# Joining two small TensorE products into one in a software-pipelined audio block

## The chip, the cores and the metric

The kernel runs on one core of a Trainium2 chip, in one launch. The metric is the device time of that launch in microseconds (us). Five instruction streams run side by side: PE (TensorE; its weight loads are listed apart as PEld), DVE (VectorE), ACT (ScalarE), POOL (GpSimd) and SP (SyncE, which here only issues DMAs). They meet through semaphores that are written out by hand.

## The reference, cut to what matters

The input is 16 sequences of 120000 samples, cut into 938 frames of 128 samples. A DCT of each frame gives 938 tokens of 128 channels; then come a decayed linear-attention layer with its MLP, and a layer with one expert for each sequence. Only the attention's scan matters here:

```
for each token t, per head (4 heads of 32 channels):
    A = lam[:, None] * A + k_t[:, None] * v_t[None, :]     # state, 32 x 32
    z = lam * z + k_t
    S_t = q_t . A ;  Z_t = q_t . z
att = S / Z
```

## The kernel before, in words

One sequence is one item `b` of a software pipeline over 16 items. Each round of the pipeline works on up to four items at different stages, and in every engine's block a function `body` writes out by hand in which order the steps of the items are issued. Tokens lie in tiles of 128 (`TILES` is 8), each tile being two blocks of 64 (`BLK`). Everything is in f32; on the trace one f32 product is two MATMUL records and two LDWEIGHTS records (a transpose is one of each).

The scan is done by blocks. Inside a block, TensorE builds the decayed scores of keys and queries (`pairs`, L1061: lines L1076, L1081 and L1086), and `scan` (L1102) multiplies them with the values (L1125). Between blocks the state is carried: for each of the first 14 blocks (`NST`) and each head, `us` (L1051) computes the block's contribution to the state, a product of the keys decayed to the block's end, `kcT` (128 tokens of a tile x 32 channels, the stationary operand), with the values. So that a product over all 128 token rows of a tile sums one block only, the values are held in two copies: `v[0]` is zero in the rows of the second block and `v[1]` in those of the first. The result goes into one PSUM bank, where element (e, i) of block i stands at column 14 e + i. DVE runs the decayed scan over the blocks in one instruction (`chain`, L813), POOL spreads it to all heads (`states`, L441), and `scan` uses it (L1118).

In each round PE issues `us` between `zts` (L1048, the denominators) and `dcts` (L1004) of the next item; behind these stand transposes (L1009), `w2s` (L1148), `ats` (L1164), `pairs(b, 2)`, and three `f1s` (L1170). SP hands the values over with two DMAs (`hand_v`, L350), before a copy of the stage's tokens (`hs`), the queries' spreads (`qx`), the way of the denominators through DRAM (`rz_dram`, `zq`) and a second copy of `hs`.

Of the kernel before, what the change touches and what calls it, by code (L numbers as in the profile page):

```python
# [10 lines left out]
P = 128  # L11
HEADS = 4
HD = P // HEADS
# [6 lines left out]
BLK = P // 2  # L20
# [31 lines left out]

def program(nc, A, out):
    B, _, full = A["xT"].shape
    T = full + 1
    TAIL = A["xtail"].shape[1]
    E = A["fc1T"].shape[0]
    TILES = -(-T // P)
    PADT = TILES * P
# [8 lines left out]
    NST = NBLK - 1  # L68
    KT = TILES - 1

    ctx = ExitStack()
    with ctx:
# [3 lines left out]
        def sb(name, *shape, dt=F32):  # L76
            return ctx.enter_context(nc.sbuf_tensor(name, [P, *shape], dt))
# [47 lines left out]
        v_f, gate_f = sb("v_f", TILES, P), sb("gate_f", PADT)  # L125
# [7 lines left out]
        kcT = sb("kcT", KT, P)  # L133
        rms_row, to_end, ends = sb("rms_row", P), sb("to_end", P), sb("ends", P)
        af = sb("af", HD * NST)

        v, gz = [sb("v_a", TILES, P), sb("v_b", TILES, P)], sb("gz", PADT)
        qx = sb("qx", 2, HEADS, QCOLS)


# [3 lines left out]
        px = [sb(f"px{i}", HEADS, BLK) for i in range(2)]  # L144
# [49 lines left out]
        def nth(b, per, n):  # L194
            return b * per + n

        def first(b):
            return isinstance(b, int) and b == 0

        def before(eng, s, b, per, n):  # L200

            if not first(b):
                eng.wait_ge(s, (b - 1) * per + n)
# [3 lines left out]
        for g in (0, 1):  # L207
# [4 lines left out]
            for j in range(4):  # L212
                emptied[f"w1_{g}{j}"] = (ge1, 8, 4 * g + j + 1)
                emptied[f"f1_{g}{j}"] = (ge2, 8, 4 * g + j + 1)
        place = {name: (i, n) for i, users in enumerate(USES) for n, (name, _) in enumerate(users)}


# [7 lines left out]
        def free_bank(pe, b, name):  # L225

            i, n = place[name]
            users, late = USES[i], USES[i][n][1]
            back = 0
            while True:  # L230
                n -= 1
                if n < 0:
                    n, back = len(users) - 1, back + 1
                who, lag = users[n]
                c = b + (late - lag - back)
                if isinstance(c, int) and c >= B:
                    continue
                if isinstance(c, int) and c < 0:
                    if b + late - back < 0:
                        break  # L240
                    continue
                s, per, count = emptied[who]
                pe.wait_ge(s, nth(c, per, count))
                break
            return bk(name)
# [46 lines left out]
        def _(sp):  # L292
# [50 lines left out]
            def hand_v(b):  # L343
                scanned, there = nth(b - 1, TILES, TILES), nth(b, 2, 2)
                if not first(b):
                    sp.wait_ge(s_out, scanned)
                sp.wait_ge(v_ok, there)
                for o in (0, 1):
                    rows = slice(BLK * o, BLK * o + BLK)
                    sp.dma_start(v[o][rows, :, :], v_f[rows, :, :]).then_inc(v_in, 16)  # L350

            def hand_gate(b):
                used, there = nth(b - 1, 2, 2), nth(b, 2, 2)
# [40 lines left out]
            def body(at):  # L394
                if (b := at(2)) is not None:
                    hand_v(b); hand_h1(b); spread(b, 1); rz_out(b); rz_back(b); hand_h2(b); spread(b, 2); spread(b, 3)
                    hand_gate(b)
                if (b := at(3)) is not None:
                    store(b, 0)
                if (b := at(0)) is not None:  # L400
                    samples(b)
                if (b := at(3)) is not None:
                    store(b, 1)
                if (b := at(2)) is not None:
                    expert(b)
                if (b := at(1)) is not None:
                    spread(b, 0)
# [265 lines left out]
        def _(dve):  # L673
            V = nc.vector
# [4 lines left out]
                V.memset(bank[i][:, :], 0.0)  # L679
            for tile in px:  # L680
                V.memset(tile[:, :, :], 0.0)
            V.memset(v[0][BLK:P, :, :], 0.0)
            V.memset(v[1][0:BLK, :, :], 0.0)
            for tile in (k, ga, gate_f, c1, xa):
                last = V.memset(tile[:, T:PADT], 0.0)
            last.then_inc(s_init, 1)
# [281 lines left out]
        def _(pe):  # L968
            mm = nc.tensor.matmul
# [81 lines left out]
            def us(b):  # L1051
                dst = free_bank(pe, b, "u")
                pe.wait_ge(kc_ok, nth(b, 1, 1))
                pe.wait_ge(v_in, nth(b, 32, 32))
                for i in range(NST):
                    for hd in range(HEADS):
                        r = slice(HD * hd, HD * hd + HD)
                        last = mm(dst[r, i:HD * NST:NST], kcT[:, i // 2, r], v[i % 2][:, i // 2, r], start=True, stop=True)  # L1058
                last.then_inc(u_ok, 1)

            def pairs(b, c):  # L1061
# [40 lines left out]
            def scan(b, c):  # L1102
                s0, S = P * (c % 4), bank[SOUT]
                if c == 0:
                    before(pe, ga_ok, b, 2, 2)
                if c == 4:
                    pe.wait_ge(ga_ok, nth(b, 2, 1))
                if c == 0:
                    pe.wait_ge(ab_ok, nth(b, 1, 1))
                    pe.wait_ge(qc_ok, nth(b, 1, 1))  # L1110
                    pe.wait_ge(v_in, nth(b, 32, 32))
                opened = False
                for o in range(blocks[c]):
                    i, t = 2 * c + o, s0 + BLK * o
                    if i:
                        for hd in range(HEADS):
                            r = slice(HD * hd, HD * hd + HD)
                            mm(S[r, t:t + BLK], ab[:, i - 1, r], qc[:, BLK * i:BLK * i + BLK], start=not opened, stop=False, skip_group_check=True)  # L1118
                        opened = True
                pe.wait_ge(px_ok, nth(b, TILES, c + 1))  # L1120
                for o in range(blocks[c]):
                    t = s0 + BLK * o
                    for hd in range(HEADS):
                        r = slice(HD * hd, HD * hd + HD)
                        last = mm(S[r, t:t + BLK], v[o][:, c, r], px[c % 2][:, hd, :], start=False, stop=True, skip_group_check=True)  # L1125
                last.then_inc(s_out, 1)

            def attends(b, g):
# [55 lines left out]
            def body(at):  # L1184
# [18 lines left out]
                if (b := at(2)) is not None:  # L1203
                    zts(b); us(b)
# [8 lines left out]
                if (b := at(2)) is not None:  # L1213
                    pairs(b, 3); scan(b, 0)
                if (b := at(3)) is not None:
                    f1s(b, 0, 3); f2s(b, 0); nmTs(b, 1)
                if (b := at(2)) is not None:
                    scan(b, 1); scan(b, 2)
# [6 lines left out]
                if (b := at(2)) is not None:  # L1225
                    scan(b, 3); pairs(b, 4)
# [65 lines left out]
```

## Time and profile before

| | |
|---|---|
| median of 3 runs | 1056.63 us (1055.34 to 1058.45) |
| the profiled execution's own time | 1056.37 us |
| its span | 1054.6 us |
| PE busy | 995.8 us (94%) |
| DVE, ACT, POOL busy | 854.4, 655.9, 343.3 us |
| PE on the chain of work that ended last | 92% |

The span is the stretch that the profiler recorded; 1.8 us of the execution's time lie outside it. "Busy" is time in which at least one instruction of the engine ran. Matmuls are pipelined: each record lasts about 0.2 us, but the next one starts some 10 ns later, so what a group of matmuls costs is read from the starts (or from the chain), not from a record's duration. A wait "<-issue" is idle time in which the engine waited for nothing that the profile shows.

### The profile page before, as it was taken

The page shows a single profiled execution, that of the slowest core. Times are in us where ns is not written, and L with a number is a line of the kernel's source. Part 1 is how long each engine was busy: PE and PEld are TensorE (multiplying, and loading weights), DVE is VectorE, ACT ScalarE, POOL GpSimd, SP SyncE. Part 2 cuts the span into 40 slices and gives each one's busy share as a digit, 9 for nine tenths or more (in the row PEclk, how much of TensorE's full clock was granted, in tenths as well). Part 3 has the DMA queues.
Part 4 walks back from the last instruction along what each step waited for, and adds up shares of the span by engine and source line. Part 5 has one row for each costly group of instructions (what it writes and reads, how often), then busy time and mean ns, then how long its engine had stood idle before and what let it go on. Part 6 is the DMA issues. An engine that isn't in the chain of part 4 may idle for free.

```text
span 1054.6 us, 48874 instructions
## 1 busy us (share of the span) xinstructions
PE 995.8 (94%) x20963; PEld 752.3 (71%) x20963; DVE 854.4 (81%) x2690; ACT 655.9 (62%) x1240; POOL 343.3 (33%) x175
## 2 busy tenths in 40 slices
PE   5579999999999999999999999997999999999987
PEld 5467776777767677777777767776677767777754
DVE  6889888888978888897888889787698888889632
ACT  3247575756757576675667657565675757667553
POOL 5142434233233424323242423334223342423220
PEclk9879999999999999999999999999999999999999
DMA  5542415242332414333251423324233251423400
GB/s 164 153 127 71 117 48 139 63 120 65 100 89 71 124 57 122 88 93 95 72 124 56 127 85 86 102 71 111 64 93 95 71 131 50 123 70 87 110 30 19
DMA packets 71638, 97.06 MB, mean 92 GB/s; under 512 B 11360, under 2 KB 46720, under 8 KB 71424
## 3 DMA queue, kind: packets, MB, share of 16 engines
q1 hardware_dynamic: 71424, 93.94, 32.1%
q8 instruction: 167, 2.74, 1.0%
q14 instruction: 47, 0.39, 0.1%
HBM read 27.89 MB, written 10.83 MB: 37 GB/s over the span
## 4 chain that ended last, share of the span: by engine, by line
PE 92%; issue 3%; DVE 2%; ACT 1%; DMA 1%; POOL 0%; SPq 0%; DVEq 0%; POOLq 0%
PE bank L1004 14%; PE bank L1148 11%; PE bank L1170 11%; PE bank L1009 10%; PE bank L1141 10%; PE bank L1176 10%; PE bank L1086 7%; PE bank L1081 4%; PE bank L1118 3%; PE bank L1125 2%; PE bank L1164 2%; PE bank L1035 2%; PE bank L1076 2%; PE bank L1058 2%; PE bank L1048 1%
## 5 line engine op out<-in xcount | busy, mean ns | idle before, releaser
L605 ACT ACTIVATE hid<-bank,f1b 128x512 f32<-128x512 f32 (+1 forms) x128 | 81.8, 652 | 146.5 <-PE bank L1170 146.1
L452 POOL TENSOR_TENSOR t_sum<-x,hs 128x512 f32<-128x512 f32 x32 | 40.8, 1273 | 370.8 <-DVE x L832 276.3
L1086 PE MATMUL bank<-qx,ki 128*32 128x16 f32 x7680 | 127.2, 192 | 7.6 <-issue 7.6
L456 POOL TENSOR_TENSOR rr<-vv,nhalf 128x8 f32<-128x8 f32 x32 | 78.5, 2454 | 151.4 <-DVE vv L713 151.4
L1148 PEld LDWEIGHTS bank<-w,hid 128*128 128x128 f32 x1024 | 118.0, 192 | 8.7 <-issue 7.2
L1170 PE MATMUL bank<-xa,f1w 128*128 128x512 f32 (+1 forms) x256 | 119.6, 582 | 1.0 <-issue 0.9
L1148 PE MATMUL bank<-w,hid 128*128 128x128 f32 x1024 | 119.6, 275 | 0.8 <-ACT hid L585 0.8
L441 POOL TENSOR_TENSOR ab<-af,heads 128x1792 f32<-128x1792 f32 x16 | 78.7, 4917 | 121.6 <-DVE af L813 121.6
L1141 PE MATMUL bank<-c,w 128*128 128x512 f32 (+1 forms) x256 | 117.0, 570 | 0.9 <-ACT c L579 0.9
L1086 PEld LDWEIGHTS bank<-qx,ki 128*32 128x32 f32 x7680 | 111.5, 110 | 8.5 <-issue 8.4
L1176 PE MATMUL bank<-hid,f2w 128*128 128x512 f32 (+1 forms) x256 | 107.5, 563 | 0.0
L882 DVE TENSOR_TENSOR ki<-k,rp 128x448 f32<-128x448 f32 (+14 forms) x256 | 93.5, 437 | 8.7 <-PE bank L1086 8.4
L1081 PE MATMUL bank<-qx,ko 128*32 128x32 f32 x2880 | 84.9, 198 | 1.9 <-issue 1.9
L1176 PEld LDWEIGHTS bank<-hid,f2w 128*128 128x128 f32 x256 | 47.4, 190 | 47.5 <-issue 47.0
L585 ACT ACTIVATE hid<-bank 128x512 f32<-128x512 f32 (+1 forms) x128 | 68.8, 562 | 16.7 <-PE bank L1141 14.9
L745 DVE SCALAR_TENSOR_TENSOR mixed<-d,vec,hl 128x938 f32<-128x938 f32 x64 | 74.5, 1184 | 0.0
L1081 PEld LDWEIGHTS bank<-qx,ko 128*32 128x32 f32 x2880 | 72.1, 112 | 2.0 <-issue 2.0
L560 ACT ACTIVATE px<-bank 128x256 f32<-128x256 f32 (+1 forms) x128 | 48.7, 381 | 39.8 <-PE bank L1125 24.8
L820 DVE COPY_PREDICATED px<-mask,bank 128x256 f32<-128x256 uint32 (+1 forms) x128 | 56.3, 442 | 14.1 <-issue 14.1
L1009 PE MATMUL bank<-ident,nl 128*128 128x128 f32 x384 | 59.0, 283 | 7.2 <-DVE nl L731 4.7
L435 POOL TENSOR_TENSOR nrm<-ssq,phalf 128x8 f32<-128x8 f32 x32 | 51.9, 1638 | 37.1 <-DVE ssq L750 37.0
L573 ACT ACTIVATE nl<-x,nb,rr 128x128 f32<-128x128 f32 x128 | 52.6, 482 | 16.0 <-DVE nb L844 16.0
(143 smaller groups left out, 2307.9 us busy)
## 6 DMA issues: line engine op xcount, KB each, us to landing
qx<-qq SPq DMA_DIRECT2D x256, 80.0 KB, 4.2
hs<-hs SPq DMA_DIRECT2D x32, 532.0 KB, 7.6
zq<-rz_dram SPq DMA_DIRECT2D x64, 128.0 KB
gz<-gate_f SPq DMA_DIRECT2D x16, 512.0 KB, 3.0
xT<-in_xT SPq DMA_DIRECT2D x16, 468.5 KB, 3.5
v_a<-v_f SPq DMA_DIRECT2D x16, 256.0 KB, 3.2
v_b<-v_f SPq DMA_DIRECT2D x16, 256.0 KB, 4.4
f1w<-in_fc1T SPq DMA_DIRECT2D x16, 256.0 KB, 2.8
```

The lines of the kernel that those rows point to most:

```text
L441: gp.tensor_tensor(ab[:, :, :].rearrange("p c (h e) -> p c h e", h=HEADS), af[:, :].rearrange("p (o e c) -> p c o e", o=1, e=HD).to_broadc ...
L456: gp.tensor_tensor(rr3[:, four(g), :], vv3[:, four(g), :], nhalf[:, 0:8].rearrange("p (m o) -> p m o", o=2), ALU.pow).then_inc(r3_ok, 1)
L605: nc.scalar.activation(hid[:, j, cols(g)], bk(f"f1_{g}{j}")[:, 0:width[g]], ACT.Gelu, bias=f1b[:, b % E, j:j + 1]).then_inc(ge2, 1)
L882: last = V.tensor_tensor(view(dst[:, 0:w]), view(k[:, HALF * g:HALF * g + w]), over(rp[:, P - ref:P - ref + n], w // m, n), ALU.mult)
L1004: last = mm(dst[:, P * i:P * i + P], src[:, P * m:P * m + P], w[:, :], start=True, stop=True)
L1009: last = nc.tensor.transpose(dst[:, P * i:P * i + P], src(m), ident[:, :])
L1081: return mm(O[r, :, t:t + EIGHT], ko[:, j - 1, s0:s0 + WIN], x[:, :, t0:t0 + EIGHT], start=True, stop=True)
L1086: return mm(D[r, :, t + j:t + WIN:EIGHT], ki[:, j, s0:s0 + WIN], x[:, :, t0 + j:t0 + WIN:EIGHT], start=True, stop=True)
L1141: mm(dst[:, 0:width[g]], w1[:, P * j:P * j + P], c1[:, cols(g)], start=True, stop=True).then_inc(w1_ok, 1)
L1148: last = mm(dst[:, P * i:P * i + P], hid[:, j, P * m:P * m + P], w2[:, j, :], start=(j == 0), stop=(j == 3))
L1170: mm(dst[:, 0:width[g]], f1w[:, P * j:P * j + P], xa[:, cols(g)], start=True, stop=True).then_inc(f1_ok, 1)
L1176: last = mm(dst[:, 0:width[g]], f2w[:, P * j:P * j + P], hid[:, j, cols(g)], start=(j == 0), stop=(j == 3))
```

## The change

The two tiles `v[0]` and `v[1]` become one tile `v` with two halves. In `us`, where each block and head had a product of its own that moved 32 columns, there is now one product for each tile and head: the same stationary keys, and as moving operand the 32 columns of either half, 64 in all. Its output is written at the same places of the bank as before. The stationary operand of L1125 and the two DMAs and memsets that fill the values only change their addresses.

```diff
-        v, gz = [sb("v_a", TILES, P), sb("v_b", TILES, P)], sb("gz", PADT)
+        v, gz = sb("v", 2, TILES, P), sb("gz", PADT)
...
-                    sp.dma_start(v[o][rows, :, :], v_f[rows, :, :]).then_inc(v_in, 16)
+                    sp.dma_start(v[rows, o, :, :], v_f[rows, :, :]).then_inc(v_in, 16)
...
-            V.memset(v[0][BLK:P, :, :], 0.0)
-            V.memset(v[1][0:BLK, :, :], 0.0)
+            V.memset(v[BLK:P, 0, :, :], 0.0)
+            V.memset(v[0:BLK, 1, :, :], 0.0)
...
-                for i in range(NST):
+                for c in range(KT):
                     for hd in range(HEADS):
                         r = slice(HD * hd, HD * hd + HD)
-                        last = mm(dst[r, i:HD * NST:NST], kcT[:, i // 2, r], v[i % 2][:, i // 2, r], start=True, stop=True)
+                        both = dst[r, 0:HD * NST].rearrange("p (e i) -> p i e", e=HD)[:, 2 * c:2 * c + 2, :]
+                        last = mm(both, kcT[:, c, r], v[:, :, c, r], start=True, stop=True)
...
-                        last = mm(S[r, t:t + BLK], v[o][:, c, r], px[c % 2][:, hd, :], start=False, stop=True, skip_group_check=True)
+                        last = mm(S[r, t:t + BLK], v[:, o, c, r], px[c % 2][:, hd, :], start=False, stop=True, skip_group_check=True)
```

On PE, the instructions around `us` in a full round stand like this before (a row is a run of like products; the shape is output partitions x moving columns, with its pieces):

```order
L1048 MATMUL bank<-zq,hsel 32x128 x8
L1058 MATMUL bank<-v_a,kcT 32x32 x4
L1058 MATMUL bank<-v_b,kcT 32x32 x4
L1058 MATMUL bank<-v_a,kcT 32x32 x4
L1058 MATMUL bank<-v_b,kcT 32x32 x4
L1058 MATMUL bank<-v_a,kcT 32x32 x4
```

There are 14 such rows of four. After the change, all of them are one row of 28 (the lines behind L1048 are one higher in the changed file), and what follows is as it was:

```order
L1048 MATMUL bank<-zq,hsel 32x128 x8
L1059 MATMUL bank<-v,kcT 32x2x32 x28
L1004 MATMUL bank<-dct,xT 128x128 x8
L1009 MATMUL bank<-ident,nl 128x128 x4
L1009 MATMUL bank<-ident,x 128x128 x4
L1149 MATMUL bank<-w,hid 128x128 x16
L1165 MATMUL bank<-c,wat 128x512
```

No instruction has changed places. Each round has 28 products, that is 56 MATMUL and 56 LDWEIGHTS records, fewer. SP's DMAs stand in the same order, with the same sizes:

```order
L341 DMA qx<-qq 32x640 x4
L350 DMA v<-v_f 64x1024 x2
L375 DMA hs<-hs 128x1064
L341 DMA qx<-qq 32x640 x4
L362 DMA rz_dram<-rz 128x128
```

Before, the second row of these was two rows, `v_a<-v_f` and `v_b<-v_f`; nothing else on SP's queue has moved.

## Rows read from the trace of the kernel before

**Rows 1.** The page: span and busy time of each engine.
```profile
span 1054.6 us, 48874 instructions
PE 995.8 (94%) x20963; PEld 752.3 (71%) x20963; DVE 854.4 (81%) x2690; ACT 655.9 (62%) x1240; POOL 343.3 (33%) x175
```

**Rows 2.** The page: engines' shares of the chain that ended last.
```profile
PE 92%; issue 3%; DVE 2%; ACT 1%; DMA 1%; POOL 0%; SPq 0%; DVEq 0%; POOLq 0%
```

**Rows 3.** PE's waits, whole span: us in total, times, longest.
```profile
PE bank L1058 <- issue: 14.4, 12, 2.5
PE bank L1086 <- issue: 7.6, 8, 3.2
...
PE bank L1004 <- issue: 2.1, 2, 1.4
...
PE bank L1081 <- issue: 1.9, 1, 1.9
PE bank L1125 <- issue: 1.6, 2, 1.2
```

**Rows 4.** PE's waits between 90 and 1000 us.
```profile
PE bank L1058 <- issue: 11.9, 11, 2.4
PE bank L1086 <- issue: 6.7, 6, 3.2
```

**Rows 5.** Timeline of PE: start, us, line, operation, records, [idle before].
```profile
536.21 0.24 PE L1058 MATMUL bank<-v_a,kcT 128*32 128x32 f32 x8
536.27 0.25 PE L1058 MATMUL bank<-v_b,kcT 128*32 128x32 f32 x8
536.34 0.23 PE L1058 MATMUL bank<-v_a,kcT 128*32 128x32 f32 x5
536.85 0.22 PE L1058 MATMUL bank<-v_a,kcT 128*32 128x32 f32 x2 [0.28 <-issue]
```

**Rows 6.** L1058 alone, its first start to the next line's: window, length, busy.
```profile
851.35:852.33 0.98, 0.98 (x112) 0.98 (x112) 1.00 0.66 171
...
975.93:977.05 1.12, 1.12 (x112) 1.04 (x112) 1.00 0.67 170
sum 33.07, PE 18.57 PEld 17.08; mean PE 1.16 PEld 1.07
```

**Rows 7.** Windows: length; PE, PEld, DVE, ACT, POOL busy (records); PEclk, DMA share, GB/s.
```profile
661.82:725.50 63.68, 61.24 (x1378) 46.58 (x1378) 52.98 (x168) 40.82 (x77) 20.89 (x10) 1.00 0.33 91
725.50:737.09 11.59, 8.37 (x125) 7.47 (x125) 8.16 (x39) 2.62 (x5) 6.61 (x3) 1.00 0.49 122
536.21:597.04 60.83, 60.55 (x1314) 45.90 (x1310) 52.59 (x167) 40.82 (x78) 20.91 (x10) 1.00 0.36 96
```

**Rows 8.** The page: the DMA queue of kind instruction (packets, MB).
```profile
q8 instruction: 167, 2.74, 1.0%
```

**Rows 9.** The chain in order of time: start, us, line, records.
```profile
851.54 0.99 PE bank L1058 x71
...
555.54 0.36 PE bank L1118 x16
...
556.13 0.22 PE bank L1118 x16
```

**Rows 10.** Timeline of PE at two idle times outside L1058.
```profile
290.04 1.16 PE L1004 MATMUL bank<-dct,xT 128*128 128x128 f32 x9 [1.44 <-issue]
...
737.09 0.51 PE L1086 MATMUL bank<-qx,ki 128*32 128x16 f32 x29 [3.22 <-issue]
```

**Rows 11.** Windows, columns as in Rows 7.
```profile
541.00:542.00 1.00, 1.00 (x12) 1.00 (x11) 0.00 (x0) 1.00 (x2) 1.00 (x1) 1.00 0.15 35
...
544.00:545.00 1.00, 1.00 (x5) 0.29 (x3) 0.69 (x1) 0.00 (x0) 0.48 (x1) 1.00 0.94 249
...
976.10:999.00 22.90, 22.90 (x587) 16.04 (x574) 15.58 (x46) 12.93 (x30) 6.57 (x2) 1.00 0.43 112
...
412.27:424.00 11.73, 10.89 (x272) 9.37 (x265) 8.58 (x34) 4.34 (x10) 5.07 (x2) 1.00 0.54 130
```

## The prediction

> **What bounds the kernel now.** I first read the page's busy times: PE is busy for 995.8 of 1054.6 us, the next engine, DVE, for 854.4 [rows 1]. Then the chain that ended last: PE has 92% of it [rows 2]. So I looked at one round, from one start of L1058 to the next: 60.83 us, of which PE is busy 60.55, DVE 52.59, ACT 40.82 [rows 7]. PE works in one unbroken stretch; what a round costs is what PE's instructions cost, plus the idle times of PE. A microsecond that PE gains in a round is a microsecond of the kernel as long as a round stays above DVE's 52.6 us, and nothing here comes near that.
>
> Next, the list of PE's waits [rows 3]. Its longest entry is L1058, the very line that is changed: 14.4 us in 12 idle times, put down to "issue", so to nothing that waits for data or a buffer. The timeline shows one [rows 5]: 8 + 8 + 5 = 21 records of L1058 run, then PE stands for 0.28 us in the middle of the group, then goes on. There is no semaphore in the middle of that loop. The 16 windows of L1058 say what the group costs: 0.98 us where it isn't interrupted, 33.07 us in all, 2.07 in the mean [rows 6].
>
> **What these idle times are.** I counted PE's records between the idle times' ends. From the one in L1058 at 661.82 to the one in L1058 at 725.50 there are 1378 matmuls and 1378 loads, from there to the one in L1086 at 737.09 there are 125 and 125 [rows 7]. 1378 is 11.02 times 125. The DMA queue of kind instruction moved 167 packets and 2.74 MB [rows 8]; 20963 matmuls [rows 1] by 167 is 125.5. So PE's instructions come in blocks of about 125 products' records with their loads, one packet each of 16.4 KB, and PE idles, if it does, where a block ends and the next has not arrived. I read them as late where their fetch meets other transfers, above all in the stretch behind L1058, where the share of the DMA engines rises from 0.15 to 0.94 within 4 us [rows 11]; the longest of all idle times, 3.22 us, comes behind that stretch of its round [rows 10]. And they are late where PE burns instructions fastest: a record of L1058 takes 0.98 us / 112 = 8.75 ns [rows 6].
>
> A round has 1314 matmul records [rows 7], 10.5 blocks. That is why L1058 is hit so often: each round the block ends move by half a block, and L1058 with 112 records is nearly a whole block long.
>
> The Trainium skill, Runtime: NRT & Kernel Launch, section "Instruction fetch mechanics", states that the instruction memory is refilled in 16 KiB blocks of 256 instructions; the 2.74 MB in 167 packets agree. By the same section the fetch is hidden, since instructions are issued slower than they are filled; the count above speaks against that here, and what would follow from it is the second rival.
>
> **The change, part by part.**
>
> *The products.* 56 of 32 columns (112 records) become 28 of 64 (56 records) in each of 16 rounds. The neighbour that does the same thing is L1118: stationary 128 x 32, moving 64 columns, four heads in turn on four column groups. 16 of its records take 0.22 us on the chain, 13.75 ns each; behind a group of another shape they take 0.36 us, 22.5 ns each [rows 9]. The lower bound is 8.75 ns, as if 64 columns cost what 32 do. I take 13.75, because all of L1059 is one run and its change of shape stays with L1048, which has the same 32-wide stationary operand: 56 x 13.75 = 0.77 us a round against 0.98 uninterrupted, bounds 0.49 and 1.26. The output of each product now comes in two pieces of 32 with the same stride of 14 elements as before; I price that at nothing (the 22.5 ns bound would hold a cost).
>
> The Trainium skill, TensorE: Matmul & The Clock Gate, section "Back-to-back issue gap", gives 1 to 64 columns one and the same price. By that rule the group would halve, 0.49 us a round and 7.8 us in all instead of 3.4. The row on L1118 beside that on L1058 says 13.75 against 8.75 ns, so I keep the row.
>
> *The idle times inside the group.* A round now has 1314 - 56 = 1258 records, and 1258 / 125.5 = 10.02 blocks. This is the other half of the change, and the larger: the block ends stop wandering and stay, in every round, at nearly the same instructions. Where? In the round at 536.21 the block ended behind 21 records of L1058. After the change the eight rounds before it have lost 8 x 56 = 448 records, so that end falls 469 records behind the group's start, and three blocks earlier (376) another falls 85 to 94 records behind it, whichever of 125 to 128 records I give a block. Behind the 56 of the group stand 16 of L1004, 8 transposes, then 32 of L1149: the end lies in L1149, not in the group. There PE starts 12 records in 1.00 us, one in 83 ns [rows 11], nearly ten times slower than in L1058. So all of the idle time in L1058 goes: 16 windows cost 16 x 0.77 = 12.3 us where they cost 33.07. That is -20.7 us, of which 3.4 from the products' own time and 17.3 from idle time.
>
> *The idle times elsewhere.* Outside L1058 the rows list 7.6 + 2.1 + 1.9 + 1.6 = 13.2 us [rows 3]. Of these 6.7 and 2.1 lie between 90 and 1000 us [rows 4], the other 4.4 at the start and the end. What takes the place of the lost ones? The next end behind L1149 is one block on, 210 to 219 records behind the group's start: behind 32 of L1149, 2 of L1165 and the 92 of one `pairs`, at the third `f1s` (L1171). Between these two ends the DMA share reaches 0.94 [rows 11]: this is the one place where a block will be late in every round. Three rounds of before bound it. In the last one L1058 is interrupted within its first records (the window 975.93 to 977.05, 1.12 us [rows 6]), so its next ends fall in L1148 and L1170, the very places of after; there PE is busy 22.90 of 22.90 us [rows 11]: nothing. In the round at 412.27 the ends lie a few records earlier, and PE is busy 10.89 of 11.73 us, so 0.84 idle, 0.3 of it in L1058 and 0.5 behind [rows 11]. In the one at 725.50 the end lies 23 records earlier in the code, in L1086, and costs 3.22 us [rows 10]. I take 0.6 us, near the two that are close in place, in 15 rounds: 9 us. For all other ends, which fall in stretches with less on the DMA engines (their mean over a round is 0.33 to 0.36 [rows 7]), 2 us. The 4.4 us at start and end stay, and since the first round's interruption (2.5 us, rows 3 less rows 4) meets a later instruction, 1 us of it is left. Sum 4.4 + 1 + 9 + 2 = 16.4 against 13.2: +3.2 us.
>
> *The rest.* One tile for two, L1126's stationary operand, the memsets and SP's two DMAs have the same sizes and places: nothing, under PE's cover. `chain` on DVE gets its bank sooner and its users don't wait for it.
>
> *The sum.* Against the profiled execution's own 1056.4 us (0.3 below the median): 1056.4 - 20.7 + 3.2 = 1038.9. I predict 1039 us.
>
> **The rivals.**
>
> *The idle time doesn't follow the count of instructions, or all of it reappears elsewhere.* Then only the products' 3.4 us go: 1053. For it: the rounds at 290.04 (1.44 us in L1004) and at 725.50 (3.22 in L1086) [rows 10] show that an end outside the group can cost as much. Against it: the counts of 125 and 1378, and that in the only uninterrupted window the group costs 0.98. It is also where the skill's "hidden" would lead: no fetch to save, 3.4 us.
>
> *The fixed places are all harmless,* as in the last round of before: the 9 and 2 us don't come. 1056.4 - 20.7 - 13.2 + 5.4 = 1028.
>
> *Locked in a bad place (slower).* One mechanism: since the ends recur at the same instruction, an end behind the heavy transfers, at L1170 and the `pairs` before it, costs in every round what it cost once, 3.22 us: 15 x 3.22 = 48 instead of 9, 1078. It decides from 15 s > 9 + 17.5, so from s = 1.8 us in a round. For it: the DMA share of 0.94; against: 0 and 0.5 us at the nearest places.
>
> *The product of two pieces is dear.* At 22.5 ns: 1.26 us a round, 8 us more, 1047. No row speaks for it.
>
> **How the numbers follow.** Forecast 0.58, with a range of its own of 1031 to 1047; nothing saved but the products 0.18; all harmless 0.11; locked and slower 0.07; dear product 0.06. A measurement of this kernel tells about 0.3% (3.2 us) from no change: below 1053.4 is faster, above 1059.8 slower. The forecast, the harmless and the dear case are faster, and half of the second rival, whose 1053 lies on the bound: 0.82 in all, allowing 0.02 for the forecast's own tail. Same 0.11, slower 0.07. For the range I leave 0.07 above and about 0.1 below and take 1028 to 1056.
>
> **What would show it.** Right: L1059 with 896 records in all, its 16 windows near 0.77 us each and without an idle time in the steady rounds; 1258 records a round; PE's remaining "issue" idle times at the same line round after round, L1171 or its neighbours, some 0.6 us each; rounds of about 60.8 us. Wrong: idle times still inside L1059; records of L1059 spaced by 8.75 or 22.5 ns; idle times of 2 us or more that recur; or PE waiting for DVE or ACT where it now waits for instructions.

## The result and the profile after

| | before | after |
|---|---|---|
| median | 1057.32 us (4 runs, 1055.34 to 1058.45) | 1026.99 us (4 runs, 1024.96 to 1028.79) |
| ratio | | 0.9716 (95% interval 0.9697 to 0.9734) |
| the profiled execution's own time | 1056.37 us | 1025.9 us |
| its span | 1054.6 us | 1024.1 us |

The kernel became 2.8% faster, 30 us, where I had predicted 18. 1027 lies just under my range of 1028 to 1056: the direction and the mechanism were right, the size was not; the outcome is that of the rival "all harmless" (1028), to which I had given 0.11.

The page of after, for [rows 1] and [rows 8]: span, busy times, and the queue that brings instructions (packets, MB).

```profile
span 1024.1 us, 47082 instructions
PE 985.9 (96%) x20067; PEld 746.1 (73%) x20067; DVE 851.6 (83%) x2690; ACT 655.8 (64%) x1240; POOL 343.2 (34%) x175
...
q8 instruction: 160, 2.62, 1.1%
```

PE's busy time fell by 9.9 us and its span by 30.5: two thirds of what was won is time in which PE did nothing before. 896 matmul records are gone and 7 packets of instructions. PE's waits in the changed kernel that are put down to "issue" (us in total, times, longest), first over the whole span, for [rows 3]:

```profile
PE bank L1087 <- issue: 4.7, 2, 4.2
PE bank L1171 <- issue: 0.9, 1, 0.9
PE bank L1177 <- issue: 0.6, 1, 0.6
```

then those of them between 90 and 1000 us, for [rows 4]:

```profile
PE bank L1177 <- issue: 0.6, 1, 0.6
PE bank L1087 <- issue: 0.5, 1, 0.5
```

Before, that list had 11.9 us in L1058 and 6.7 in L1086. The joined products don't appear at all. The 0.9 us ahead of the first L1171 of the last round (at 1003.09 us) is no late block: every run here has an idle time of 0.89 us at that instruction (before at 1033.55), wherever its blocks end. In the middle of the run they look like this (timeline: start, us, line, records), for [rows 5]:

```profile
522.94 0.64 PE L1048 MATMUL bank<-zq,hsel 128*32 128x128 f32 x16
523.40 0.96 PE L1059 MATMUL bank<-v,kcT 128*32 128x64 f32 x56
524.29 2.05 PE L1004 MATMUL bank<-dct,xT 128*128 128x128 f32 x16
```

From 523.40 to 524.29, so 0.89 us to the first start of the next line, without a gap. For the same stretch before I had taken 0.98 from [rows 6], but that window ended at the last start of L1058; the next line began later:

```profile
850.90 0.63 PE L1048 MATMUL bank<-zq,hsel 128*32 128x128 f32 x14
...
852.45 0.71 PE L1004 MATMUL bank<-dct,xT 128*128 128x128 f32 x4
```

The round from one start of the group to the next, for [rows 7] (length; PE, PEld, DVE, ACT, POOL busy; clock; DMA share):

```profile
523.40:583.93 60.53, 60.52 (x1258) 45.82 (x1254) 52.45 (x167) 40.81 (x78) 20.87 (x10) 1.00 0.33 96
```

PE is busy 60.52 of 60.53 us. PE remains the bound, and nothing else has come forward. The 60.53 us are one of 14 full rounds, which take 60.2 to 60.5 us each but for one of 60.9.

### The profile page after: what moved, and what is told of

It is laid out like the page before. It is cut to its first block, busy times and chain, and to the rows that moved or that the text cites. A ratio compares the mean times of both kernels' runs of the same rounds, so it can differ in the third digit from the quotient of the medians.

```text
span 1024.1 us, 47082 instructions
## 1 busy us (share of the span) xinstructions
PE 985.9 (96%) x20067; PEld 746.1 (73%) x20067; DVE 851.6 (83%) x2690; ACT 655.8 (64%) x1240; POOL 343.2 (34%) x175
## 4 chain that ended last, share of the span: by engine, by line
PE 94%; DVE 2%; DMA 1%; ACT 1%; issue 1%; POOL 0%; SPq 0%; DVEq 0%; ACTq 0%; POOLq 0%
PE bank L1004 14%; PE bank L1149 11%; PE bank L1171 11%; PE bank L1142 10%; PE bank L1009 10%; PE bank L1177 10%; PE bank L1087 8%; PE bank L1082 4%; PE bank L1119 3%; PE bank L1126 3%; PE bank L1165 2%; PE bank L1035 2%; PE bank L1077 2%; PE bank L1059 1%; PE bank L1048 1%
## 5 line engine op out<-in xcount | busy, mean ns | idle before, releaser
L1087 PE MATMUL bank<-qx,ki 128*32 128x16 f32 x7680 | 127.1, 192 | 4.7 <-issue 4.7
L1149 PEld LDWEIGHTS bank<-w,hid 128*128 128x128 f32 x1024 | 118.0, 192 | 8.7 <-issue 7.2
L1149 PE MATMUL bank<-w,hid 128*128 128x128 f32 x1024 | 119.6, 275 | 0.8 <-ACT hid L585 0.8
L1171 PE MATMUL bank<-xa,f1w 128*128 128x512 f32 (+1 forms) x256 | 118.0, 576 | 1.0 <-issue 0.9
L1087 PEld LDWEIGHTS bank<-qx,ki 128*32 128x32 f32 x7680 | 112.0, 110 | 5.1 <-issue 4.9
L1177 PE MATMUL bank<-hid,f2w 128*128 128x512 f32 (+1 forms) x256 | 107.6, 563 | 0.6 <-issue 0.6
L1177 PEld LDWEIGHTS bank<-hid,f2w 128*128 128x128 f32 x256 | 47.4, 190 | 48.3 <-issue 47.8
L585 ACT ACTIVATE hid<-bank 128x512 f32<-128x512 f32 (+1 forms) x128 | 68.8, 562 | 17.2 <-PE bank L1142 15.7
L820 DVE COPY_PREDICATED px<-mask,bank 128x256 f32<-128x256 uint32 (+1 forms) x128 | 56.4, 442 | 13.9 <-issue 13.9
L1142 PEld LDWEIGHTS bank<-c,w 128*128 128x128 f32 x256 | 42.7, 190 | 27.7 <-issue 25.7
```

The costliest lines, as they stand in the source:

```text
L1087: return mm(D[r, :, t + j:t + WIN:EIGHT], ki[:, j, s0:s0 + WIN], x[:, :, t0 + j:t0 + WIN:EIGHT], start=True, stop=True)
L1142: mm(dst[:, 0:width[g]], w1[:, P * j:P * j + P], c1[:, cols(g)], start=True, stop=True).then_inc(w1_ok, 1)
L1149: last = mm(dst[:, P * i:P * i + P], hid[:, j, P * m:P * m + P], w2[:, j, :], start=(j == 0), stop=(j == 3))
L1171: mm(dst[:, 0:width[g]], f1w[:, P * j:P * j + P], xa[:, cols(g)], start=True, stop=True).then_inc(f1_ok, 1)
L1177: last = mm(dst[:, 0:width[g]], f2w[:, P * j:P * j + P], hid[:, j, cols(g)], start=(j == 0), stop=(j == 3))
```

## The experiments

Two theories were to be told apart. Mine: PE's instructions arrive in blocks, PE idles where a block ends before the next one has landed, and what the change did above all is to fix the block ends at harmless places of the round. The rival: shorter work and fewer instructions explain it, wherever blocks end. The eleven kernels ran in three groups (e1 to e4, e5 to e8, e9 to e11), each on one chip with the kernel before beside it; its median there stands with each result. The changed kernel wasn't timed again in these groups, so differences from its 1026.99 us also hold what the chips differ by: the kernel before took 1054.25 to 1057.32 us on them. Each trace is of one run, and its idle times are that run's.

**Moving the block ends, with the work unchanged (e1).** On PE, before the first round:

```diff
+                for _ in range(4):
+                    mm(spare[E % len(spare)][0:HD, 0:E], wnext[:, 0:HD], fc2b[:, :], start=True, stop=True)
                 mm(spare[E % len(spare)][:, 0:E], wnext[:, :], fc2b[:, :], start=True, stop=True).then_inc(s_gp, 1)
```

> The changed kernel with four tiny products (128 x 32 stationary, 8 moving columns, overwritten by what follows) added once, on PE, in the first microseconds of the program, where it waits anyway; nothing else differs. They add 16 instructions ahead of the first round and move every end of an instruction block 16 instructions earlier in every round. My theory (PE idles where a block of instructions ends before the next has arrived, and the place of the ends decides): the second end behind the joined products moves from the last records of the third f1s (L1171 of the changed kernel), some 10 us behind the group's start, to the end of the dense pairs group ahead of it, 7 us behind it. The block then arrives 1.3 to 2.4 us late in each of 15 rounds: 1045 to 1060 us, with idle times <-issue in the pairs lines (L1087, here L1089) in nearly every round. Rival (the place of the ends doesn't matter, fewer instructions do): within 1 us of the changed kernel, 1027 to 1028.

Measured: 1052.47 us (before 1056.87; ratio 0.9964, 0.9933 to 0.9996). Four tiny products at the start of the program take back 25 of the 30 us. The trace is of the fastest of ten runs, which took 1046.37 us; the others go up to 1057.74. PE's idle times in steady rounds are all at one instruction (timeline of PE, [idle before]):

```profile
179.07 0.27 PE L1128 MATMUL bank<-px,v 128*32 128x64 f32 x2 [1.42 <-issue]
242.13 0.27 PE L1128 MATMUL bank<-px,v 128*32 128x64 f32 x2 [2.61 <-issue]
304.31 0.27 PE L1128 MATMUL bank<-px,v 128*32 128x64 f32 x2 [1.58 <-issue]
...
547.91 0.27 PE L1128 MATMUL bank<-px,v 128*32 128x64 f32 x2 [1.42 <-issue]
...
609.04 0.27 PE L1128 MATMUL bank<-px,v 128*32 128x64 f32 x2 [0.60 <-issue]
...
795.75 0.27 PE L1128 MATMUL bank<-px,v 128*32 128x64 f32 x2 [3.07 <-issue]
```

Eleven idle times, 14.4 us, each ahead of the last two records of the same group. The time came as expected, the place did not: I had named the second block end behind the joined products (in `pairs`), it is the third, in `scan` (L1126 of the changed kernel). Counting between two of these idle times also mends a count of mine:

```profile
547.91:609.04 61.13, 60.52 (x1251) 45.75 (x1251) 52.07 (x166) 40.79 (x77) 20.15 (x11) 1.00 0.32 92
609.04:669.79 60.75, 60.51 (x1250) 45.75 (x1250) 52.15 (x167) 40.79 (x77) 20.56 (x11) 1.00 0.33 94
```

A round is 1250 or 1251 records of either kind, exactly ten times the 125 of [rows 7]; the 1258 of a window that opens in running work counts the records still in flight. The ends don't wander at all.

**The same count with narrower products (e2).** The kernel before, with

```diff
-                for i in range(NST):
+                for i in range(0, NST, 2):
```

> The kernel before with only the products of the even blocks in its state step: 28 products of 32 columns a round (the odd blocks' contributions are left out of the computation). It has the instruction count of the changed kernel, with moving operands half as wide. Theory: block ends in the same places as in the changed kernel, so the same few idle times; the group costs 56 x 8.75 = 0.49 us a round in place of 56 x 13.75 = 0.77, so 4.5 us less than the changed kernel, about 1022.5. Rival (up to 64 columns cost the same): same as the changed kernel, 1027. Rival (the gain is from wider products keeping PE busy, not from the count): idle times stay and it stays above 1045.

Measured: 1022.05 us (before 1056.87; ratio 0.9679, 0.9656 to 0.9701), against 1022.5 expected. 4.9 us less than the changed kernel, 0.31 us a round for half the columns. The groups themselves show it too, 0.63 us from the first start of L1058 to that of the next line, against 0.89. So the price of 64 columns is not that of 32, and the instruction count alone, without any wider product, brings the whole effect on the idle times. Its waits <-issue between 90 and 1000 us, of which the 0.9 is the one that every kernel has:

```profile
PE bank L1170 <- issue: 0.9, 1, 0.9
...
PE bank L1086 <- issue: 0.3, 1, 0.3
```

**Letting the ends wander again (e3).**

```diff
-                for c in range(KT):
+                for c in [*range(KT), KT - 1]:
```

> The changed kernel with the last tile's four joined products issued twice in every round (same operands, same output): 16 instructions more a round, 2576 in place of 2560, so the block ends are no longer fixed but move 16 instructions earlier with each round. The work added is 8 records of 13.75 ns, 0.11 us a round, 1.8 us in all. Theory: the ends sweep over dense places, PE idles again in 6 to 10 of the rounds by 1 to 2 us each: 1027 + 1.8 + 8 to 18 = 1037 to 1047. Rival (the count alone matters): 1029.

Measured: 1047.70 us (before 1056.87; ratio 0.990, 0.986 to 0.994), 20.7 us above the changed kernel for 1.8 us of work and slightly more than I had expected. The trace is of the slowest of six runs, 1053.02 us. The idle times are spread over lines again (the four largest of PE's waits <-issue between 90 and 1000 us):

```profile
PE bank L1087 <- issue: 8.7, 7, 2.4
PE bank L1082 <- issue: 3.6, 2, 2.1
PE bank L1059 <- issue: 3.6, 5, 1.3
PE bank L1004 <- issue: 1.4, 1, 1.4
```

**Fewer bytes on the DMA engines, in the kernel before (e4).** For both copies, here the first:

```diff
-                sp.dma_start(hs1[:, :], hs0[:, :]).then_inc(hs1_in, 16)
+                n = hs0.shape[1] if first(b) else 8
+                sp.dma_start(hs1[:, 0:n], hs0[:, 0:n]).then_inc(hs1_in, 16)
```

> The kernel before, but from the second sequence on the two hand-over copies of hs (532 KB each) move 8 of 1064 columns (the later stages then work on stale tokens; the amount of work is unchanged). Theory (instruction blocks arrive late because their fetch stands behind these copies on the DMA engines): the idle times <-issue fall from 29.8 us to about 12 to 18, the time to 1039 to 1047. Rival (the block's own latency is what is late, whatever else the DMA engines do): 1055 to 1058.

Measured: 1039.73 us (before 1056.87; ratio 0.9836, 0.9793 to 0.9878). The block ends wander as before, but the waits <-issue between 90 and 1000 us fall from 21 us (11.9 and 6.7 [rows 4], 2.4 in smaller entries) to 7.6:

```profile
PE bank L1060 <- issue: 4.0, 2, 2.2
PE bank L1088 <- issue: 1.9, 3, 0.8
PE bank L1006 <- issue: 1.7, 2, 1.5
```

Between 90 and 1000 us all of PE's waits in the kernel before are put down to "issue", so it waits there neither for the copies nor for anything they feed. What they do is make instruction blocks late. They aren't the only cause: 7.6 us are left.

**A bad place on purpose (e5).** As e1, with 32 tiny products.

> The changed kernel with 32 of the tiny products (128 instructions) added once on PE ahead of the first round, so that every block end lies 128 instructions earlier in the round than in the changed kernel: 45, 301 and 557 instructions behind the start of the joined products. Theory (the place of the fixed ends decides): ends fall in dense groups with the DMA engines busy, and from the places and the delays seen so far I work out 2.5 to 3.8 us of idle time in each of 15 rounds: 1060 to 1085 us, so slower than the kernel before although it does less. Rival (the gain of the change is its shorter work and count, the shift by 16 was a special case): 1027 to 1040.

Measured: 1059.14 us, the median of eight of its nine runs; the ninth took 1073.50 us (before 1054.25; ratio 1.0047, 1.0016 to 1.0079). It has the joined products, and it is about 5 us slower than the kernel before. It lies just under the range that I had worked out, and about 3 us of it are the tiny products: its first joined product starts at 49.84 us, that of the changed kernel at 46.77. Between 90 and 1000 us:

```profile
PE bank L1089 <- issue: 16.5, 15, 2.9
PE bank L1061 <- issue: 6.8, 8, 1.2
```

**A slightly better place (e6).** As e1, with 61 tiny products.

> The changed kernel with 61 tiny products (244 instructions) ahead of the first round: the ends lie 12 instructions later than in the changed kernel (244 of 256 earlier is 12 later). Theory: the ends keep clear of the dense groups with a little more room than in the changed kernel; the added products cost up to 1 us once; 1023 to 1029 us, no idle time <-issue between 90 and 1000 us. Rival (adding this many products at the start harms by itself): above 1032.

Measured: 1031.64 us (before 1054.25; ratio 0.9785, 0.9766 to 0.9804). My figure for the time failed, since I had priced the tiny products at 1 us. The first joined product starts 6.2 us later than in the changed kernel:

```profile
52.94 0.99 PE L1061 MATMUL bank<-v,kcT 128*32 128x64 f32 x56 [0.58 <-DMA v<-v_f]
```

The part on the place held: of the waits <-issue between 90 and 1000 us 0.2 us are left. From the first joined product to the end of the span it takes 1029.6 - 52.94 = 976.7 us, the changed kernel 1024.1 - 46.77 = 977.3. With 0.2 us of idle time left, there is next to nothing more to be had from the place of the ends in the steady rounds.

**Bad place, thin copies (e7).** e1 with the copies of e4.

> The kernel of e1 (ends 16 instructions earlier than in the changed kernel, 1052 us) with the two hand-over copies of hs moving 8 of 1064 columns from the second sequence on (later stages work on stale tokens, their amount of work is unchanged). Theory (a block is late because its fetch stands behind these copies): the idle time in L1128 goes, 1026 to 1034. Rival (other transfers, the queries' spreads, are what the fetch stands behind): 1042 or more.

Measured: 1028.90 us (before 1054.25; ratio 0.9753, 0.9734 to 0.9771). Without the copies the bad place costs next to nothing; the 14.4 us of e1 are 1.3 here:

```profile
PE bank L1130 <- issue: 1.3, 3, 0.6
```

**The control (e8).** The kernel before with e5's 32 tiny products.

> The kernel before with the same 32 tiny products at the start as e5. Its block ends wander over the round anyway (2672 instructions a round), so by the theory the shift only changes which rounds are hit: 1050 to 1064. Rival (the tiny products themselves, or the shift of the first rounds, cost tens of us): above 1070.

Measured: 1063.42 us (before 1054.25; ratio 1.008, 1.0061 to 1.0098), 9 us above before and within the expected range. Its first L1060 starts at 50.75 us, 2.9 later than before, so about 3 us are the tiny products themselves and 6 the different rounds that are hit. e5 beside it, with the same additions and the joined products, is 4.3 us faster: at this place little more than the products' own work is won.

**Is a block 256 instructions? (e9, e10, e11).** The changed kernel with 61, 64 and 68 tiny products as PE's very first work:

```diff
             pe.wait_ge(s_dct, 16)
+            for _ in range(64):
+                mm(spare[0][0:HD, 0:8], dct[:, 0:HD], dct[:, 0:8], start=True, stop=True)
```

> The changed kernel with 61 tiny products (244 instructions) as in e6, but as the very first work of PE, while it waits some 5 us for the samples anyway. The block ends lie 12 instructions later than in the changed kernel, and the products' own time (in e6 the first joined product started 6.2 us later) is covered. Theory: 1023 to 1027 us, at best 3 us under the changed kernel's 1027, from the 1.1 us of idle time that it has behind 90 us and a PE clock that rises earlier. Rival (the products delay the start here too): 1029 or more.

> The same with 64 tiny products, 256 instructions: by the theory, that a block holds 256 instructions, the ends then lie exactly where they lie in the changed kernel, and the time is the changed kernel's, 1024 to 1029 us, with PE's idle times <-issue between 90 and 1000 us under 3 us. Rival (a block is some other number of instructions): idle times as in e1 or e5, above 1040.

> The same with 68 tiny products, 272 instructions. By the theory 272 is 256 + 16, so this kernel must behave like e1, where 16 were added: 1044 to 1058 us, with its idle times in the product of values and scores (the line L1126 of the changed kernel, three lines further down here). Rival (the 16 of e1 hurt for another reason, such as the start): within 3 us of the run with 64.

Measured, with before at 1055.89 us: e9 1031.20 us (ratio 0.9767, 0.9715 to 0.9819), e10 1031.71 us (0.9763, 0.972 to 0.9807), e11 1058.47 us (1.0015, 0.9987 to 1.0043). The times of e9 and e10 missed, because the tiny products are not covered: 128 records take 7.00 us there (timeline of e10), and the first joined product starts at 52.91 us, 6.1 later than in the changed kernel.

```profile
2.65 7.00 PE L1002 MATMUL bank<-dct 128*32 128x8 f32 x128 [2.65 <-DMA dct<-in_dct]
```

No kernel with moved ends beats the change. But the question they were made for is answered. PE's waits <-issue between 90 and 1000 us, of e10 and of e11:

```profile
PE bank L1089 <- issue: 0.2, 1, 0.2
```

```profile
PE bank L1128 <- issue: 17.8, 12, 2.9
```

256 added instructions leave the ends where they are, 272 act like the 16 of e1, on the same line and in about the same size, and cost 27 us against 256. Only four tiny products, of four instructions each, separate e10 from e11.

The counts agree to the instruction. The first line of the page of e10, and of that of e11:

```profile
span 1030.0 us, 47337 instructions
...
span 1058.4 us, 47353 instructions
```

That is 255 and 271 more than the 47082 of the changed kernel: PE's stream lost one separate semaphore wait (at 4.9 us, L1014 of the changed kernel) when the tiny products were put ahead of it. An end should then lie one instruction later in the round than in e1, and it does: here one record of the group is left behind each of the twelve idle times, in e1 two. Two of the twelve (timeline of e11):

```profile
370.19 0.24 PE L1128 MATMUL bank<-px,v 128*32 128x64 f32 x1 [2.88 <-issue]
...
497.34 0.24 PE L1128 MATMUL bank<-px,v 128*32 128x64 f32 x1 [0.88 <-issue]
```

The list of waits doesn't hold all that a late block costs. Behind four of the twelve, those of 2.88, 1.80, 2.25 and 2.61 us, the clock granted to PE falls to half (1.2 instead of 2.4 GHz) for 3.4 us (windows, columns as in [rows 7]; the clock is the number behind POOL's):

```profile
370.80:374.20 3.40, 3.40 (x5) 1.33 (x4) 3.24 (x14) 2.28 (x6) 0.00 (x0) 0.51 0.38 156
435.70:439.10 3.40, 3.40 (x5) 1.33 (x4) 3.04 (x12) 2.04 (x5) 0.00 (x0) 0.50 0.39 159
```

From the idle time's end at 370.19 to the next group's start it takes 48.44 us, from the one at 497.34, behind which the clock stays, 46.83. So a fall costs 1.6 us on top of the idle time. In the trace of before there is one, behind the 3.22 us of [rows 10], and in that of e1 one, behind the 3.07 us; one of 2.61 us in e1 had none. The traces of the changed kernel and of e10 have none between 90 and 1000 us. The one of before:

```profile
738.60:742.00 3.40, 3.40 (x11) 0.87 (x13) 0.00 (x0) 1.39 (x3) 1.40 (x1) 0.50 0.02 5
```

## Why the prediction was right and where it was wrong

*The bound.* Right. PE was and is the bound; its idle time goes into the time at least one to one (e11 shows 1.6 us more where the clock falls behind it), and DVE with 52.45 us of a round of 60.53 never came near.

*The products' own time.* Right: I said 3.4 us. From the first start of the group to that of the next line it fell from 1.10 us (851.35 to 852.45) to 0.89, 0.21 a round or 3.4 us. The row on L1118 was the right neighbour, and e2 shows the same from the other side. The rule of the Trainium skill that 1 to 64 columns cost the same (TensorE: Matmul & The Clock Gate, "Back-to-back issue gap") would have given 7.8, and the rows of e2 and of after speak against it.

*The idle time inside the group.* Right: I said 17.3 us. Of PE's time, the 16 groups with their idle times (first start to the next line's) took 35.0 us before and 14.4 after, 20.6 less where I said 20.7, so 17.2 for the idle time. The waits put down to L1058 are gone, and the mechanism, blocks of instructions whose ends are fixed by a round of a whole number of blocks, is shown by e1, e3, e10 and e11. The rival with 1053, that all of it reappears elsewhere, did not come true here, but e5 is that case: it happens when the ends are fixed elsewhere. So the "locked in a bad place" rival was not a fancy either; its place was only not the one of this kernel.

*The idle time elsewhere.* This is the step that failed, by its size. I let 13.2 us become 16.4, with 9 us for "the next end behind L1149 [...] at the third `f1s`" and 2 for all others. Measured: the waits <-issue sum to 6.2 us, of which 1.1 lie between 90 and 1000 us, not 11. The end that I feared shows no idle time in any round, and the one behind it 0.55 us, once:

```profile
298.10 2.31 PE L1177 MATMUL bank<-hid,f2w 128*128 128x512 f32 x5 [0.55 <-issue]
```

That is 10.2 of the 13 us by which the forecast misses the profiled execution (1038.9 against 1025.9). Another 2.2 us come from the other side of the term: the 13.2 us of before were too few, since the list [rows 3] goes on with two waits that I left out of the sum,

```profile
PE bank L1048 <- issue: 1.3, 1, 1.3
PE bank L1170 <- issue: 0.9, 1, 0.9
```

so the waits elsewhere fell from 15.4 to 6.2 us where I had them rise from 13.2 to 16.4. The rest, under 1 us, I haven't taken apart; the clock's fall at 738.60, which after doesn't have, is in it. What I did wrong is plain from the rows that I had: the last round of before had its ends in the very lines in which they lie after, and showed no idle time [rows 11]. I gave it the same weight as the round at 412.27 and let the one at 725.50 pull the value up, because they lay "a few records earlier" and 23 records earlier. (It was 31: the second end of after lies two records into the third `f1s`, one block of 125 ahead of the one at 298.10, and the end at 737.09 had 29 records of L1086 still ahead of that line.) But a few records are not a small distance here. 16 instructions are what separates 1027 from 1052 us (e1): with them an end leaves the slow records of L1177, which take about 0.43 us each, for the dense group ahead of it, and is reached over two microseconds sooner: 13.9 us behind the group's start in e1 (at 304.31, idle time left out), 16.1 in the changed kernel (at 298.10). How near two places are must be measured in time on PE, not in records.

*The start.* I let 5.4 us stand at the start and end; 5.1 are there (4.2 in L1087, 0.9 in L1171). That they agree is in part luck: before had 8.7 us there in seven idle times, and I had counted 6.9.

*The block's size.* I used 125.5 matmul records and found 10.02 blocks a round. It is 125 with their 125 loads, 1250 a round (the rest of the 256 are waits for semaphores); before it was 1306, since a window also counts the records still in flight at its start. By the same slip I read 83 ns for a record of L1149 from the 12 of a window of 1 us [rows 11]; 32 of them take 3.57 us from the first start to the next line's (285.11 to 288.68 in after), 0.11 us each. Neither moves the forecast. The Trainium skill's 256 instructions (Runtime: NRT & Kernel Launch, "Instruction fetch mechanics") agree with e10 and e11. Its statement beside it, that the fetch is hidden, fits most of the blocks but not all: 17 idle times with 18.6 us stand in the two entries of [rows 4], against 167 packets [rows 8], and 14.4 us in e1.

*What stays open.* That the fetch stands behind other transfers is shown by e4 and e7 for the two copies of `hs` as far as this: with them made thin, blocks are late less often and by less. Whether the fetch waits in line behind a copy or shares the engines with it, no run tells apart, nor was the changed kernel run with thin copies alone. Why one and the same end is late by 3.07 us in one round and not at all in another (e1) is open too. So is why the third end is the one that suffers in e1 and not the second; no run tells it apart.

## What to carry to other kernels

Where an engine that bounds the kernel idles "<-issue" in the middle of a group, count its instructions between such idle times: if the counts are multiples of one number, its instruction blocks arrive late, and then the instructions of a round modulo that number, and where in the round the block ends fall, can be worth more than the work that a change saves. A change of a few instructions far away can then give or take 2 to 3 per cent (e1, and e11 against e10), so compare kernels by their idle times at block ends too before you credit an edit with a gain. And bulk copies that nobody waits for still cost if they stand before the fetch of instructions.

## What the runs showed of the hardware that I had not expected

- 16 added instructions before the first round cost 25 us (1052.47 against 1026.99), 272 act like 16 and 256 like none, apart from their own 5 us.
- A kernel with fewer and wider products was no faster than the one before (e5, 1059.14 against 1054.25, some 3 us of it its tiny products; e8, with the same tiny products and the products of before, took 1063.42).
- Two copies of 532 KB for which PE never waits cost 17 us through late instruction blocks (e4, 1039.73 against 1056.87).
- A tiny product (32 columns stationary, 8 moving) costs PE 7.00 us / 64 = 0.11 us among the first work of the program.
- The runs of a kernel whose ends lie at harmless places agree better: 1030.98 to 1034.08 us in e6 and 1020.96 to 1023.24 in e2, against 1046.37 to 1057.74 in e1 and 1055.19 to 1065.11 in e5 without its slowest. The four of e8, whose ends wander, lie close too (1061.44 to 1064.20).
- Behind four late blocks of 1.80 to 2.88 us the granted clock fell to 0.50 for 3.4 us (e11); each fall cost about 1.6 us more.
